# One attention loop over 128 heads: each head cut into four equal quarters, with the query projection moved to another bank

## The reference

```python
q = (q_c @ Wq_up.T + bq_up).reshape(b, s, NH, Q_HEAD).transpose(0, 2, 1, 3)
scores = jnp.einsum('bhqd,bhkd->bhqk', q, k) / np.sqrt(Q_HEAD)
attn = jax.nn.softmax(scores, axis=-1)
o = jnp.einsum('bhqk,bhkv->bhqv', attn, v)
out = jnp.einsum('bhsv,Hv->bsH', o, Wo) + bo
```

## Time and profile before

| | |
|---|---|
| median of three executions | 2102.14 us (2101.27 to 2105.47) |
| profiled execution, own time | 2104.11 us |
| its span, first to last instruction | 2100.8 us, mean granted TensorE clock 0.992 |
| busy share of TensorE, VectorE, ScalarE, GpSimd | 95%, 79%, 70%, 25% |

### The profile page before, as it was taken

How to read it: one execution, slowest core, us unless ns; L and a number is a source line. 1 busy time by engine, 2 the same in 40 slices (tenths; PEclk the granted TensorE clock), 3 DMA queues, 4 the chain that set the end, 5 groups by cost and what they waited for, 6 DMA issues and landing times. The chain is left out here.

```text
span 2100.8 us, 37011 instructions
## 1 busy us (share of the span) xinstructions
PE 1994.5 (95%) x11014; PEld 1543.3 (73%) x11014; DVE 1652.9 (79%) x2716; ACT 1480.0 (70%) x2616; POOL 517.9 (25%) x831
## 2 busy tenths in 40 slices
PE   7999999999999999999999999999999999999799
PEld 6777777777777777777777777777777777777577
DVE  6588887888878888788877888878888788887665
ACT  4477777777777777777777777777777777777534
POOL 3312222222222222222222222222322222222320
PEclk9899999999999999999999999999999999999899
DMA  5511111111111111111211111111111111111201
GB/s 201 196 30 31 39 40 31 39 33 39 40 32 39 31 39 40 31 39 32 39 38 33 39 31 39 40 31 39 33 39 39 32 39 31 39 34 37 76 22 59
DMA packets 123461, 95.18 MB, mean 45 GB/s; under 512 B 75009, under 2 KB 97569, under 8 KB 123425
## 3 DMA queue, kind: packets, MB, share of 16 engines
q1 hardware_dynamic: 119328, 86.33, 16.1%
q0 software_dynamic: 4096, 8.40, 2.1%
HBM read 83.95 MB, written 10.75 MB: 45 GB/s over the span
## 5 line engine op out<-in xcount | busy, mean ns | idle before, releaser
L812 ACT ACTIVATE PTH<-X 128x512 fp32r<-128x512 f32 x1024 | 568.2, 595 | 343.3 <-PE X L696 338.7
L871 DVE TENSOR_TENSOR PTL<-X,PTH 128x512 f16<-128x512 f32 x1024 | 700.5, 684 | 8.5 <-ACT PTH L812 1.2
L887 DVE TENSOR_REDUCE mx<-S 128x1 f32<-128x1024 f32 x512 | 622.2, 1215 | 93.9 <-PE S L718 93.4
L828 ACT ACTIVATE prob<-S,shift 128x1024 f32<-128x1024 f32 x512 | 571.5, 1116 | 126.3 <-DVE shift L894 120.9
L696 PE MATMUL X<-ident,prob 128*128 128x128 f32 x4096 | 592.4, 272 | 0.7 <-DVE PTL L871 0.7
L696 PEld LDWEIGHTS X<-ident,prob 128*128 128x128 f32 x4096 | 499.6, 140 | 96.0 <-issue 5.0
L716 PE MATMUL S<-kvTH,qeH 128*128 128x512 f32 x1024 | 439.4, 429 | 1.8 <-DVE qeL L876 1.6
L718 PE MATMUL S<-kvTH,qeL 128*128 128x512 f32 x1024 | 405.1, 396 | 0.0
L717 PE MATMUL S<-kvTL,qeH 128*128 128x512 f32 x1024 | 403.5, 394 | 0.0
L662 POOL TENSOR_TENSOR onormLH<-onorm,onormH 64x512 fp32r<-64x512 f32 x128 | 163.4, 1276 | 839.9 <-ACT onormH L839 839.9
L727 PE MATMUL O<-PTH,kvn 128*128 128x512 f32 x1024 | 364.0, 437 | 0.0
(11 more groups left out here) (201 smaller groups left out, 1890.7 us busy)
## 6 DMA issues: line engine op xcount, KB each, us to landing
recip_row<-row_scratch SPq DMA_DIRECT2D x128, 256.0 KB, 5.1
weff<-weff_scratch SPq DMA_DIRECT2D x128, 192.0 KB, 5.0
wv<-in_wv POOLq DMA_DIRECT2D x128, 64.0 KB
raw<-in_raw SPq DMA_DIRECT2D x8, 772.0 KB, 6.8
weff_scratch<-w_split SPq DMA_DIRECT2D x8, 768.0 KB, 4.9
x<-in_x SPq DMA_DIRECT2D x4, 1024.0 KB, 6.9
x_all<-in_x SPq DMA_DIRECT2D x3, 1024.0 KB, 6.4
out<-y SPq DMA_DIRECT2D x3, 1024.0 KB, 4.2
```

Source lines behind the costliest of these rows:

```text
L812: nc.scalar.activation(PTH[p][:, 4 * part:4 * part + 4, u * P:(u + 1) * P], X[:, bank(g, k, par), :].rearrange("p (k c) -> p k c", k=4), A ...
L828: nc.scalar.activation(prob[u][:], S[:, u % 2, :], ACT.Exp, bias=shift[:, col:col + 1], accum_out=rs[:, col:col + 1]).then_inc(probs_ready, 1)
L871: v.tensor_tensor(PTL[p][at], X[:, bank(g, k, par), :].rearrange("p (k c) -> p k c", k=4), f32(PTH[p][at]), ALU.subtract).then_inc(low_out, 1)
L887: v.reduce_max(mx[:, col:col + 1], S[:, u % 2, :], AX.X).then_inc(max_ready, 1)
```

## The change

The bodies of all engines are ordered anew in four quarters u = 0 to 3.

- TensorE: `scores(u)`, eight transposes of one unit, and then, by quarter: the next head's query projection (0), five high value matmuls (1), three high value matmuls and the two matmuls into `V` (2), the eight low value matmuls (3). All sixteen value matmuls of a head now stand in one body.
- The query projection writes into `O`, the bank of the value sum, in place of a bank of `X`. It waits for `onorm_ready`, since `onorm` reads `O`. It has semaphores of its own (`q_filled`, `q_high`, `q_low`), and `X` has eight fills a head; `event` is 8g + k - 3 and `bank` is gone.
- ScalarE: `exp(u)` moves from behind the copies of quarter u to behind the copies of quarter u + 1; that of unit 3 stands in quarter 0 of the next body. `high_q` stands at the head of quarter 1. `onormH` moves to the end of quarter 0, `onormLH` to the end of quarter 1.
- VectorE: `onorm` moves from ahead of quarter 1 to ahead of quarter 0. The reciprocal moves from behind quarter 0 to ahead of quarter 2. `low_q` stands ahead of quarter 1.
- SyncE's body is as before but for the wait ahead of the weight load.

```diff
 def event(g, k):
-    if isinstance(g, int):
-        if g == -1:
-            return 1
-        if g == NG or (g == NG - 1 and k > 6):
-            return 9 * g + k - 3
-    return 9 * g + k - 2
-
-
-def bank(g, k, par):
-    return event(g, k) % 2 if isinstance(g, int) else (par + k) % 2
+    return 8 * g + k - 3
...
-                sp.wait_ge(x_filled, event(g - 3, 6))
+                sp.wait_ge(q_filled, g - 1)
...
+                def next_queries():
                     if not isinstance(g, int) or g >= 2:
                         pe.wait_ge(onorm_ready, g - 1)
...
+                    project_queries(g + 1, (g + 1) // NH if isinstance(g, int) else b, 1 - par)
+
+                for u in range(UN):
+
+                    if on:
+                        scores(u)
+                    if (one, on)[u // 2]:
+                        pe.wait_ge(probs_ready, 4 * g + u - 1)
+                        transposes(g, 2 * u, (u + 2) % UN)
+                        transposes(g, 2 * u + 1, (u + 2) % UN)
+                    if u == 0 and on and exists(g + 1):
+                        next_queries()
...
+                    if u == 1 and one:
+                        if exists(g + 1) and on:
+                            pe.wait_ge(q_low, g + 2)
+                        pe.wait_ge(high_out, event(g, 2))
+                        pv_high(0, 4)
+                        pe.wait_ge(high_out, event(g, 3))
+                        pv_high(4, 5)
+                    if u == 2 and one:
+                        pv_high(5, KEYT)
+                    if u == 2 and two:
+
+                        pe.wait_ge(wv_split, g - 1)
+                        pe.wait_ge(onorm_high, 2 * g - 2)
+                        pe.wait_ge(onorm_low, g - 1)
+                        mm(V[:], wvH[par][:], onormH[:], start=False, stop=False)
+                        mm(V[:], wvHL[par][:], onormLH[:], start=False, stop=isinstance(h, int) and h == 1).then_inc(wv_done, 1)
+                    if u == 3 and one:
+                        pe.wait_ge(low_out, event(g, 3))
+                        pv_low()
...
+                for u in range(UN):
+                    if u == 1 and on and exists(g + 1):
+                        high_q(g + 1, h + 1 if not isinstance(g, int) else (h + 1) % NH, 1 - par)
+                    if (one, on)[u // 2]:
+                        high(g, 2 * u, (u + 2) % UN, (1 - par, par)[u // 2])
+                        high(g, 2 * u + 1, (u + 2) % UN, (1 - par, par)[u // 2])
+                    if u == 0 and one:
+                        exp(g - 1, 3, 1 - par)
+                    if u > 0 and on:
+                        exp(g, u - 1, par)
...
+                for u in range(UN):
+                    if u == 0 and two:
                         dve.wait_ge(pv_done, g - 1)
                         dve.wait_ge(row_in[par], 16 * turns(g - 2, par))
                         if not isinstance(g, int) or g >= 3:
                             dve.wait_ge(wv_done, g - 2)
                         v.tensor_tensor(onorm[:], O[:], recip_row[par][:], ALU.mult).then_inc(onorm_ready, 1)
...
+                    if u == 1 and on and exists(g + 1):
+                        low_q(g + 1, h + 1 if not isinstance(g, int) else (h + 1) % NH, 1 - par)
+                    if u == 2 and one:
                         dve.wait_ge(probs_ready, 4 * g)
                         if not isinstance(g, int) or g >= 3:
                             dve.wait_ge(recip_out, 16 * (g - 2))
                         v.reciprocal(recip[:, (1 - par) * UN:(2 - par) * UN],
                                      rs[:, (1 - par) * UN:(2 - par) * UN]).then_inc(recip_ready, 1)
```

More of the change, by code:

```diff
@@ L545, in attention @@
          wv_split, onorm_high, onorm_low, ffn_in, row_ready, bo_added, projected0, summed0,
[L546 removed]
+         stats0, std0_done, q_filled, q_high, q_low) = (sem(n) for n in names)
         ident = keep["ident"]
@@ L673, in free_bank, with transposes @@
+            def transposes(g, k, unit):
                 if not isinstance(g, int) or event(g, k) > 2:
                     pe.wait_ge(low_out, event(g, k) - 2)
[L675 to L690, removed]
@@ L692, in transposes @@
-            def transposes(g, par, unit, k, part):
-                out = free_bank(g, k, par)
                 for j in range(4):
-                    last = nc.tensor.transpose(out[:, j * P:(j + 1) * P],
-                                               prob[unit][:, (4 * part + j) * P:(4 * part + j + 1) * P], ident[:])
+                    tile = 4 * (k % 2) + j
+                    last = nc.tensor.transpose(X[:, k % 2, j * P:(j + 1) * P], prob[unit][:, tile * P:(tile + 1) * P], ident[:])
                 last.then_inc(x_filled, 1)
-            block_now = [0]
@@ L719, in scores, with pv_high @@
                     last.then_inc(scores_ready, 1)
-                def pv(back, first, end):
-                    batch = ((g - back) // NH if isinstance(g, int) else b) // 2
-                    i = par if back == 2 else 1 - par
+                def pv_high(first, end):
                     for kt in range(first, end):
[L727 to L734, removed]
@@ L737, in body @@
[L737 to L754, removed]
@@ L755, in body @@
[L755 to L768, removed]
@@ L769, in body, with pv_low @@
-                if one:
+                        mm(O[:], keep["kvn"][:, batch * KEYT + kt, :], PTH[1 - par][:, kt, :], start=(kt == 0), stop=False)
+                def pv_low():
+                    for kt in range(KEYT):
+                        half = slice(kt % 2 * KVL, (kt % 2 + 1) * KVL)
+                        ins = mm(O[half, :], keep["kv16"][:, batch * KEYT + kt, :], PTL[1 - par][:, kt, :],
+                                 start=False, stop=(kt >= KEYT - 2))
+                    ins.then_inc(pv_done, 1)
@@ L783, in body @@
[L783 to L794, removed]
@@ L795, in body @@
-                if on:
-                    transposes(g, par, 1, 8, 1)
+                    project_queries(g + 1, (g + 1) // NH if isinstance(g, int) else b, 1 - par)
[8 more added lines that the diff above has]
+                        next_queries()
+                    if u == 1 and isinstance(g, int) and g == NG:
+                        pe.wait_ge(vsum_out, 1)
+                        pe.wait_ge(ffn_in, 16 * 9)
+                        for t in range(UN):
+                            mm(projection[t], keep["vsum"][:, t * P:(t + 1) * P], keep["wo"][:],
+                               start=True, stop=True).then_inc(projected0, 1)
+                    if u == 1 and one:
[16 more added lines that the diff above has]
+                        pv_low()
@@ L809, in _, with high @@
         def _(act):
-            def high(g, k, par, u, part, p):
+            def high(g, k, unit, p):
                 act.wait_ge(x_filled, event(g, k))
[L812 to L818, removed]
@@ L820, in _, with high_q @@
-            high_q(-1, 0, 1)
+                part = 4 * (k % 2)
+                nc.scalar.activation(PTH[p][:, part:part + 4, unit * P:(unit + 1) * P],
+                                     X[:, k % 2, :].rearrange("p (k c) -> p k c", k=4), ACT.Copy).then_inc(high_out, 1)
+            def high_q(nxt, h, i):
+                act.wait_ge(q_filled, nxt + 1)
+                nc.scalar.activation(qeH[i][:], O[:], ACT.Identity, bias=keep["beff"][:, ds(h, 1)]).then_inc(q_high, 1)
+            high_q(0, 0, 0)
@@ L822, in body, with exp @@
             def body(g, b, h, par):
[L823 to L827, removed]
+                on, one, two = exists(g), exists(g - 1), exists(g - 2)
+                def exp(head, u, i):
+                    col = i * UN + u
+                    act.wait_ge(shift_ready, 4 * head + u + 1)
                     nc.scalar.activation(prob[u][:], S[:, u % 2, :], ACT.Exp, bias=shift[:, col:col + 1],
@@ L839, in body @@
                         nc.scalar.activation(onormH[:], onorm[:], ACT.Copy).then_inc(onorm_high, 1)
[L840 to L848, removed]
+                    if u == 1 and two:
+                        nc.scalar.activation(onormLH[KVL:P, :], onorm[0:KVL, :], ACT.Copy).then_inc(onorm_high, 1)
                 if isinstance(g, int) and g == NG + 1:
@@ L895, in negated @@
                                            op0=ALU.add, op1=ALU.subtract, reverse1=True).then_inc(shift_ready, 1)
-                for u in range(2):
-                    if u == 1 and two:
+                for u in range(UN):
+                    if u == 0 and two:
                         dve.wait_ge(pv_done, g - 1)
```

101 lines of the change are left out of this document (39 added, 62 removed).

## The result

The changed kernel takes 3110.64 us in the median of four executions (3107.34 to 3124.06), against 2102.5 us before: a ratio of 1.480, 95% interval 1.476 to 1.485. The forecast was 3098 us, slower. The profiled execution has 3112.47 us.

What follows compares the result with a forecast made beforehand. The reciprocals' way through DRAM ends last: a head takes 20.8 us plus 1.6 for the lower clock, 22.4 in place of 14.56. 127 x 7.84 = 996 us on 2104.1 gives 3100, forecast 3098 us; range 2830 to 3220.

Steps and rivals of the forecast that it cites:

- The bank of X: TensorE's query projection no longer waits for VectorE to free a bank: 0.80 us a head, 102 us to be gained.
- Transposes in eights, value matmuls together: TensorE's regrouped transposes and value matmuls: costed at nothing; without TensorE's new idle time up to 0.3 us a head.
- The exponential behind the copies: ScalarE's new order: scores, transposes, two copies and exponential make a quarter at least 4.24 us, against TensorE's 3.44.
- The reciprocal and onorm: VectorE's ring of one head: 14.6 us from reciprocal to row, plus onorm, quarters 0 and 1 and low_q, 20.81 us.
- The way: From VectorE's reciprocal through DRAM (store, then load on SyncE's queue) to the row for onorm: 14.6 us, ends 12.8 and 15.5.
- the weight load: On SyncE's queue behind the row's load: its data come about 0.5 us after the row, within onorm's 0.69; costs nothing.
- The clock: TensorE pauses some 3 us a head, so its clock falls in most heads: 1.6 us a head, ends 0 and 2.5.
- 1: Rival: the way through DRAM bounds but TensorE's clock stays up, 2898 us; chance 0.23.
- 2: Rival: TensorE's clock stays low throughout, 23.3 us a head, 3214 us; chance 0.12.
- 3: Rival: the row comes in time, the store landing in about 2 us, and ScalarE's ring bounds, 2414 us; chance 0.07.
- 4: Rival: faster, TensorE's 13.76 us a head bound, 2002 us; chance 0.02.
- ScalarE's ring: Per quarter, six score matmuls, transposes, two copies and the exponential in turn: 4.24 us, four of them 17.0 us a head.

Runs made afterwards that it cites:

- Experiment 9: Reciprocal behind quarter 0, exponential and weight load early, short store; against that kernel, quarter 1's transposes split around scores(1) and one value matmul moved: 2000.19 us, ratio 0.9521.
- experiment 2: Changed kernel with normalization by the row sums left out and the weight load moved ahead of the reciprocal's store: 2466.48 us.
- experiment 3: Changed kernel with only the exponential back ahead of the two copies: 3005.91 us, then 2997.85 us beside its control at 2938.46 us.
- Experiment 7: Changed kernel with the reciprocal back behind quarter 0: alone 2474.02 us; with the exponential ahead of the copies and the weight load ahead of the store, 2345.24 us.
- experiment 1: Changed kernel with onorm multiplying by a ready tile of ones, so normalization is left out and it waits for no row: 2886.66 us.
- experiment 4: Changed kernel with eight extra 512-column matmuls a head filling TensorE's pause before the projection, result unchanged: 2867.25 us.

## Why the prediction was right

**The bank of X** was costed at 0.80 us a head and TensorE's other work at 13.76. Experiment 9 has 13.78 us a head with the projection in O and the rings named above out of the way. So a gain of that size is there, and the changed kernel could not show it; that the bank alone makes it is inferred from the sum, since no run moves the projection alone.

**Transposes in eights, value matmuls together,** costed at nothing: true for the time of the matmuls, but with them a value matmul came right behind the transposes that feed it, and that wait is 0.42 us a head (14.20 against 13.78). It was not named. It lay in the slack of the changed kernel and cost nothing there.

**The exponential behind the copies,** 4.24 us a quarter: 4.36 measured in experiments 2 and 7. It is the second ring; quarters 2 and 3 of the changed kernel itself take 4.36 us too, and by experiment 3 undoing it alone gains nothing.

**The reciprocal and onorm,** 14.6 + 6.21 = 20.81 us: 20.73 in the head shown, 20.84 on the mean of the 5 heads at full clock. The way was 14.47 us on the mean of all heads, and VectorE's part 6.44 where the clock stayed up; there one `negated` took 0.47 us and not 0.21. Experiment 7 shows that undoing the reciprocal's place takes back 464 us. By experiments 1 and 2 the weight load is next in line: costed at nothing, it lands only some 0.4 us before the projection starts, and takes the row's place as soon as the row is gone. In the changed kernel itself it did cost nothing.

**The clock,** 1.6 us a head with the ends 0 and 2.5: 1.62 measured, from few heads, and 1.4 in the later executions. Experiment 4 shows by adding work that the low clock is part of the loss and comes with the pause. TensorE's pause was put at some 3 us and is 3.8. The rule of the Trainium skill ("TensorE: Matmul & The Clock Gate", section on oscillation) that a loop which waits for a transfer each turn runs at the lower clock in part now has a steady loop that agrees with it: 122 of 127 heads have a low stretch. The sign given for it, PEclk well below 9 through the attention, came out weaker: the slices read 8 or 9.

**The sum** was 12.6 us under the measured median. The mechanism was right, but a hit this close is luck: the way was put 0.13 us too long and the rest of a head, 6.21 + 1.6, 0.2 too short (8.0 measured), and later, on two chips, the same kernel took 2938 and 2942 us, 5% under the forecast and within its range, by a shorter way through DRAM. The way of 14.6 was read from a trace that had the same long way. Two slips in the working move nothing: eleven matmuls at 0.20 us are 2.2 us, not 2.1, and the lower end of the range, (20.3 - 14.56) x 127, is 729 us and needs the 2104 added, which gives 2833. The rivals: 1 (2898 us) is what heads at full clock would give; 2 did not come, the clock rises again in nearly every head; 3 failed by its store, for which SyncE still waits 8.9 us; 4 (2002 us) came true only in experiment 9 (2000.19 us), with the reciprocal and the exponentials back in their old order, a short store and split transposes.

## What to carry to other kernels

Before a producer or a consumer is moved, write down for each pair that is tied by a transfer how long the way takes and how much time the old order left between them; a wait list that shows almost nothing (12.9 us here) may mean a way that fits by a tenth of a microsecond. In this loop of in-order queues one late transfer stopped everything behind its consumer, and then the clock fell too (1.4 to 1.6 us a head), so the loss was larger than the lateness. When one wait is removed, count the next ones before giving up: here the row, the weight load, ScalarE's ring and one local wait had to go, and only then did what was left of the change pay 4.8%.

## What the runs showed of the hardware

- A store of 512 single numbers of 4 bytes keeps SyncE waiting for 8.1 to 9.2 us on the mean in the kernels before and after; the same 512 numbers in 16 runs of 128 bytes take 2.5 us with the issue of four transfers. The Trainium skill ("DMA: Bandwidth & Descriptors", section on the anatomy of one DMA) has about 2 us for the fixed cost of a transfer issued from GpSimd; these are issued from SyncE. The second is near that figure, the first is four times it.
- The way from the reciprocal to `onorm` in the changed kernel was 14.5 us on the mean in the first profile and 13.4 in two later ones, on two chips, with the kernel before at 2101 to 2103 us each time. A kernel bound by it should be compared only with a control run beside it.
- VectorE turns a [128 x 32] tile by blocks in 0.21 us, once a head.
- Work that nobody needs made the kernel faster (experiment 4), by keeping the clock up.
